# A graph layer's convolution by frequencies: the shared product in fp32, the other factors' sums from the table, three buffers

## What is computed

```python
h = relu(bn1(conv1d(h, conv1_w)))            # one tap
h = bn2(conv1d(h, conv2_w, pad=8))           # 17 taps over the 256 nodes, 256 -> 256 channels
x_conv = relu(h + x)
x_nmp  = exp(-dist(x)) @ relu(x @ w_msg.T + b_msg)
gi = concat(x_conv, x_nmp) @ w_ih.T + b_ih   # then the gates of a GRU cell
```

## Time and profile before

| | |
|---|---|
| median of three runs | 1865.35 us |
| the profiled execution, its own time | 1863.11 us |
| its span in the profile | 1861.2 us |
| PE busy | 1794.3 us (96%) |
| PE weight loads busy | 1603.6 us (86%) |
| DVE busy | 1296.5 us (70%) |
| ACT busy | 1058.2 us (57%) |
| POOL busy | 972.0 us (52%) |
| DMA moved | 262.65 MB |

### The profile page before, as it was taken

The page is one execution under the profiler, slowest core; times in us unless marked ns, Lnnn a source line. Parts: engine busy times, 40 slices in busy tenths (PEclk is TensorE's granted clock), DMA queues, the critical chain, the costliest instruction groups (busy, mean ns, idle before and its releaser), DMA issues.

```text
span 1861.2 us, 31300 instructions
## 1 busy us (share of the span) xinstructions
PE 1794.3 (96%) x10736; PEld 1603.6 (86%) x10736; DVE 1296.5 (70%) x2316; ACT 1058.2 (57%) x1883; POOL 972.0 (52%) x1092
## 2 busy tenths in 40 slices
PE   5999999999999998999879999999999999999998
PEld 5999999999999998999768888888888888888886
DVE  8899999999888729999984454454455455445444
ACT  5998989989898876666543233233333323323322
POOL 6788888888767629999951222122122122212211
PEclk9999999999999999999989999999999999999999
DMA  6465665656555355665754534544443453454442
GB/s 199 140 213 190 206 197 197 209 189 212 203 187 183 136 160 133 146 168 145 191 156 123 118 78 102 119 83 102 114 92 93 113 114 80 104 119 82 101 109 40
DMA packets 513819, 262.65 MB, mean 141 GB/s; under 512 B 365575, under 2 KB 473479, under 8 KB 513662
## 3 DMA queue, kind: packets, MB, share of 16 engines
q1 hardware_dynamic: 512606, 260.52, 50.9%
q10 hardware_dynamic: 1056, 0.13, 0.0%
HBM read 151.51 MB, written 109.05 MB: 140 GB/s over the span
## 4 chain that ended last, share of the span: by engine, by line
PE 84%; DVE 6%; issue 4%; POOL 3%; DMA 2%; ACT 1%; SPq 0%; DVEq 0%; POOLq 0%; ACTq 0%
PE P L114 70%; PE P L936 5%; PE P L619 4%; PE P L646 3%; PE P L638 1%; DVE yo L829 1%; DVE wh0l L774 1%; DMA y_d<-yo 1%; POOL xsum L727 1%; PE P L667 1%; DVE wsum L755 1%; DVE wh1l L774 1%; POOL xh1l L745 0%; ACT mt L817 0%; DVE wgl L893 0%
## 5 line engine op out<-in xcount | busy, mean ns | idle before, releaser
L918 POOL TENSOR_TENSOR xnx1l<-xnf,xnx1h 128x1024 fp32r<-128x1024 f32 x16 | 44.4, 2773 | 344.3 <-ACT xnx1h L911 344.3
L918 POOL TENSOR_TENSOR xnx0l<-xnf,xnx0h 128x1024 fp32r<-128x1024 f32 x15 | 41.6, 2774 | 318.4 <-ACT xnx0h L911 318.4
L1017 ACT ACTIVATE tr<-P,cold 128x512 f32<-128x512 f32 x64 | 44.2, 690 | 194.2 <-PE P L114 194.2
L1020 ACT ACTIVATE nn<-gn,col 128x512 f32<-128x512 f32 x64 | 46.4, 725 | 179.3 <-DVE gn L1034 179.3
L1041 DVE SCALAR_TENSOR_TENSOR tz<-tz,tr 128x512 f32<-128x512 f32 x64 | 44.3, 692 | 147.9 <-ACT tz L1024 147.8
L549 POOL TENSOR_TENSOR axl<-af,axh 128x512 fp32r<-128x512 f32 x64 | 92.2, 1441 | 99.4 <-ACT axh L375 99.4
L1024 ACT ACTIVATE tz<-P,cold 128x512 f32<-128x512 f32 x64 | 44.0, 688 | 162.1 <-PE P L114 162.1
L1030 DVE SCALAR_TENSOR_TENSOR gn<-tr,gn 128x512 f32<-128x512 f32 x64 | 44.2, 690 | 127.3 <-ACT tr L1017 127.3
L114 PE MATMUL P<-w1mh,xxh 128*128 128x512 f32 x256 | 108.0, 422 | 0.0
L936 PEld LDWEIGHTS P<-gt,yt 128*128 128x128 f32 x768 | 98.8, 189 | 6.8 <-DMA yt<-y_d 1.9
L936 PE MATMUL P<-gt,yt 128*128 128x136 f32 (+1 forms) x768 | 100.9, 281 | 1.5 <-DMA yt<-y_d 1.5
(11 more groups left out here) (227 smaller groups left out, 7119.7 us busy)
## 6 DMA issues: line engine op xcount, KB each, us to landing
xh_d<-xst SPq DMA_DIRECT2D x64, 320.0 KB, 4.9
xl<-xh_d SPq DMA_DIRECT2D x40, 512.0 KB, 6.2
y_d<-yo SPq DMA_DIRECT2D x80, 256.0 KB, 2.4
x<-in_x SPq DMA_DIRECT2D x64, 256.0 KB, 3.0
a<-in_adj SPq DMA_DIRECT2D x64, 256.0 KB, 4.2
at<-in_adjt SPq DMA_DIRECT2D x64, 256.0 KB, 4.6
x_d<-x SPq DMA_DIRECT2D x64, 256.0 KB, 4.7
xn_d<-xt SPq DMA_DIRECT2D x64, 256.0 KB, 4.8
```

Of the source, the lines that this page charges most:

```text
L918: e.e.tensor_tensor(o[1][:, :, :], xnf[p % 2][:, :, :, :].rearrange("p c i t -> p c (i t)"), o[0][:, :, :], ALU.subtract).then_inc(done, 1)
L1020: e.e.activation(nn[:, :], gn[:, :], ACT.Tanh, bias=n_b[:, o:o + 1]).then_inc(S["nn"], 1)
```

## The change

The common product is no longer made of split operands: it is one fp32 matmul for each c, of `xsum` and `wsum` themselves, two in place of six. The sums' high and low parts go away (`xsh`, `wsh` semaphores, L735, L745, L764, L774), and `xh`, `wh` hold two quantities in place of three. The table now gives -(wr + wi) and wi - wr, both factors of the other two products; `wsum` is -1 times the first minus the second, which is 2 wr, so the copy out of PSUM multiplies by 0.5. `wh`, `xsum` and `wsum` have three buffers, `yo` four. Both chunks' copies to `mt` are on ACT. `spectra_sum` and `weights_sum` wait for the bin that last used their buffer, no longer for the splits. The common product now comes before the waits for the split operands and for `ye`. The filter's operands are made two bins ahead, at the end of a turn.

```diff
-        v = np.cos(2 * np.pi * k * f / NT)
-        if im:
-            v = np.sin(2 * np.pi * k * f / NT) - v
+        re, imag = np.cos(2 * np.pi * k * f / NT), np.sin(2 * np.pi * k * f / NT)
+        v = re if f in (0, NF) else imag - re if im else -imag - re
...
-        xh = [p2.hl(f"xh{i}", [128, 3, 2, 256]) for i in range(3)]
-        wh = [p2.hl(f"wh{i}", [128, 3, 2, 256]) for i in range(2)]
-        xsum = p2("xsum", [128, 32, 16])
-        wsum = p2("wsum", [128, 2, 256])
+        xh = [p2.hl(f"xh{i}", [128, 2, 2, 256]) for i in range(3)]
+        wh = [p2.hl(f"wh{i}", [128, 2, 2, 256]) for i in range(3)]
+        xsum = [p2(f"xsum{i}", [128, 2, 256]) for i in range(3)]
+        wsum = [p2(f"wsum{i}", [128, 2, 256]) for i in range(3)]
         mt = [p2(f"mt{i}", [128, 256]) for i in range(2)]
-        yo = [p2(f"yo{i}", [128, 512]) for i in range(2)]
+        yo = [p2(f"yo{i}", [128, 512]) for i in range(4)]
...
         def spectra_sum(e, f):
+
             e.wait_ge(S[f"lxh{f // 2 % 2}"], 2 * loaded(f // 2, 2))
-            e.wait_ge(S["xslo"], f - 1)
-            e.wait_ge(S["xshi"], f - 1)
+            e.wait_ge(S["frq"], 2 * f - 4)
             x = bin_of(f)
-            e.e.tensor_tensor(xsum[:, :, :], x[:, 0], x[:, 1], ALU.add).then_inc(S["xsum"], 1)
+            e.e.tensor_tensor(xsum[f % 3][:, :, :].rearrange("p c (g t) -> p (c g) t", g=16), x[:, 0], x[:, 1],
+                              ALU.add).then_inc(S["xsum"], 1)
 
         def spectra_hi(e, f):
             e.wait_ge(S[f"lxh{f // 2 % 2}"], 2 * loaded(f // 2, 2))
             e.wait_ge(S["frq"], 2 * f - 4)
-            e.e.copy(parts_of(xh[f % 3][0]), bin_of(f)).then_inc(S["xhi"], 1)
-            if f:
-                e.wait_ge(S["xsum"], f)
-                e.e.copy(sum_of(xh[f % 3][0]), xsum[:, :, :]).then_inc(S["xshi"], 1)
+            e.e.copy(by_group(xh[f % 3][0]), bin_of(f)).then_inc(S["xhi"], 1)
 
         def spectra_lo(e, f):
             h, l = xh[f % 3]
             e.wait_ge(S["xhi"], f + 1)
             e.wait_ge(S["frq"], 2 * f - 4)
-            e.e.tensor_tensor(parts_of(l), bin_of(f), parts_of(h), ALU.subtract).then_inc(S["xlo"], 1)
-            if f:
-                e.wait_ge(S["xshi"], f)
-                e.wait_ge(S["xsum"], f)
-                e.e.tensor_tensor(sum_of(l), xsum[:, :, :], sum_of(h), ALU.subtract).then_inc(S["xslo"], 1)
+            e.e.tensor_tensor(by_group(l), bin_of(f), by_group(h), ALU.subtract).then_inc(S["xlo"], 1)
 
         def weights_of(f):
             return wf[f // 10 % 2][:, 2 * (f % 10):2 * (f % 10) + 2, :, :]
 
         def weights_sum(e, f):
             e.wait_ge(S["wev"], UNITS * (f // 10 + 1))
-            e.wait_ge(S["wslo"], f - 1)
-            e.wait_ge(S["wshi"], f - 1)
+            e.wait_ge(S["frq"], 2 * f - 4)
             w = weights_of(f)
-            e.e.scalar_tensor_tensor(out=wsum[:, :, :], in0=w[:, 0, :, :], scalar=-2.0, in1=w[:, 1, :, :],
+            e.e.scalar_tensor_tensor(out=wsum[f % 3][:, :, :], in0=w[:, 0, :, :], scalar=-1.0, in1=w[:, 1, :, :],
                                      op0=ALU.mult, op1=ALU.subtract).then_inc(S["wsum"], 1)
 
         def weights_hi(e, f):
             e.wait_ge(S["wev"], UNITS * (f // 10 + 1))
-            e.wait_ge(S["frq"], 2 * f - 2)
-            e.e.copy(wh[f % 2][0][:, 0:2, :, :], weights_of(f)).then_inc(S["whi"], 1)
-            if f:
-                e.wait_ge(S["wsum"], f)
-                e.e.copy(wh[f % 2][0][:, 2, :, :], wsum[:, :, :]).then_inc(S["wshi"], 1)
+            e.wait_ge(S["frq"], 2 * f - 4)
+            e.e.copy(wh[f % 3][0][:, :, :, :], weights_of(f)).then_inc(S["whi"], 1)
 
         def weights_lo(e, f):
-            h, l = wh[f % 2]
+            h, l = wh[f % 3]
             e.wait_ge(S["whi"], f + 1)
-            e.wait_ge(S["frq"], 2 * f - 2)
-            e.e.tensor_tensor(l[:, 0:2, :, :], weights_of(f), h[:, 0:2, :, :], ALU.subtract).then_inc(S["wlo"], 1)
-            if f:
-                e.wait_ge(S["wshi"], f)
-                e.wait_ge(S["wsum"], f)
-                e.e.tensor_tensor(l[:, 2, :, :], wsum[:, :, :], h[:, 2, :, :], ALU.subtract).then_inc(S["wslo"], 1)
+            e.wait_ge(S["frq"], 2 * f - 4)
+            e.e.tensor_tensor(l[:, :, :, :], weights_of(f), h[:, :, :, :], ALU.subtract).then_inc(S["wlo"], 1)
 
 
         def main(chunk):
@@ -782,51 +762,46 @@
 
         def freq(e, f, chunk):
 
+
             n = 2 * f + chunk
+            xb, wb = xh[f % 3], wh[f % 3]
+
+            def product(o, q, k):
+                return multiply(e.e, mm3([{c: x[:, q, c, 128 * chunk:128 * chunk + 128] for c in range(2)} for x in xb],
+                                         [{c: w[:, k, c, :] for c in range(2)} for w in wb],
+                                         o, True, True, [(0, 0), (1, 1)]))
+
+            if f:
+                e.wait_ge(S["xsum"], f)
+                e.wait_ge(S["wsum"], f)
+                e.wait_ge(S["mt"], n - 3)
+                for c in range(2):
+                    t = e.e.matmul(common(chunk)[:, 0:256], xsum[f % 3][:, c, 128 * chunk:128 * chunk + 128],
+                                   wsum[f % 3][:, c, :], start=c == 0, stop=c == 1, skip_group_check=True)
+                t.then_inc(S["com"], 1)
             e.wait_ge(S["xhi"], f + 1)
             e.wait_ge(S["xlo"], f + 1)
             e.wait_ge(S["whi"], f + 1)
             e.wait_ge(S["wlo"], f + 1)
             e.wait_ge(S["ye"], n - 1)
-            e.wait_ge(S[f"mt{chunk}"], f - 1)
-            xb, wb = xh[f % 3], wh[f % 2]
-
-            def product(o, q, k):
-                return multiply(e.e, mm3([{c: x[:, q, c, 128 * chunk:128 * chunk + 128] for c in range(2)} for x in xb],
-                                         [{c: w[:, k, c, :] for c in range(2)} for w in wb],
-                                         o, True, True, [(0, 0), (1, 1)]))
-
-            if f == 0:
-                product(main(chunk)[:, 0:256], 0, 0)
-                product(main(chunk)[:, 256:512], 1, 1).then_inc(S["frq"], 1)
-                return
-            e.wait_ge(S["xshi"], f)
-            e.wait_ge(S["xslo"], f)
-            product(common(chunk)[:, 0:256], 2, 0).then_inc(S["com"], 1)
-            product(main(chunk)[:, 256:512], 0, 1)
-            e.wait_ge(S["wshi"], f)
-            e.wait_ge(S["wslo"], f)
-            product(main(chunk)[:, 0:256], 1, 2).then_inc(S["frq"], 1)
+            product(main(chunk)[:, 0:256], 1 if f else 0, 0)
+            product(main(chunk)[:, 256:512], 0 if f else 1, 1).then_inc(S["frq"], 1)
 
         def common_out(e, f, chunk):
-
             n = 2 * f + chunk
             e.wait_ge(S["com"], n - 1)
             e.wait_ge(S["ye"], n - 1)
-            if chunk == 0:
-                e.e.copy(mt[0][:, :], common(0)[:, 0:256]).then_inc(S["mt0"], 1)
-            else:
-                e.e.tensor_copy(mt[1][:, :], common(1)[:, 0:256]).then_inc(S["mt1"], 1)
+            e.e.mul(mt[chunk][:, :], common(chunk)[:, 0:256], 0.5).then_inc(S["mt"], 1)
 
         def freq_out(e, f, chunk):
             n = 2 * f + chunk
             e.wait_ge(S["frq"], n + 1)
-            e.wait_ge(S[f"sy{chunk}"], 16 * f)
+            e.wait_ge(S[f"sy{n % 4}"], 16 * (n // 4))
             if f == 0:
-                e.e.tensor_copy(yo[chunk][:, :], main(chunk)[:, :]).then_inc(S["ye"], 1)
+                e.e.tensor_copy(yo[n % 4][:, :], main(chunk)[:, :]).then_inc(S["ye"], 1)
                 return
-            e.wait_ge(S[f"mt{chunk}"], f)
-            e.e.tensor_tensor(yo[chunk][:, :].rearrange("p (q o) -> p q o", q=2),
+            e.wait_ge(S["mt"], n - 1)
+            e.e.tensor_tensor(yo[n % 4][:, :].rearrange("p (q o) -> p q o", q=2),
                               main(chunk)[:, :].rearrange("p (q o) -> p q o", q=2),
                               mt[chunk][:, :].unsqueeze(1).broadcast_to((128, 2, 256)),
                               ALU.add).then_inc(S["ye"], 1)
...
 
         def load_y(e, b):
             e.wait_ge(S["idf"], b - 2)
-            e.wait_ge(S[f"sy{b // 32}"], 16 * NF)
+            for n in (b // 32, b // 32 + 2):
+                e.wait_ge(S[f"sy{n}"], 16 * (2 * NF // 4))
             e.e.dma_start(yt[b % 3][:, 0:2, :], y_all[4 * NT * b:4 * NT * b + 384].rearrange(
...
                 unit_out(e, n)
-            weights_hi(e, 0)
+            for f in range(2):
+                weights_hi(e, f)
             for n in range(UNITS, UNITS + AHEAD):
                 unit_out(e, n)
             spectra_hi(e, 1)
             for f in range(NF):
-                if f + 1 < NF:
-                    weights_hi(e, f + 1)
                 if f:
                     common_out(e, f, 0)
                 if f + 2 < NF:
                     spectra_hi(e, f + 2)
                 for n in units_in(f, 0):
                     unit_out(e, n)
+                if f:
+                    common_out(e, f, 1)
                 for n in units_in(f, 1):
                     unit_out(e, n)
+                if f + 2 < NF:
```

(24 more changed lines are left out.)

## The result

The changed kernel took 1836.71 us (median of 4 runs, 1835.93 to 1838.8) against 1864.89 us of the kernel before in the same comparison: 0.9848 of its time, 95% interval 0.9831 to 0.9865. Forecast were 1836 us and a faster kernel. The span of the profiled execution went from 1861.2 to 1834.8 us, 26.4 us less; forecast were 29. (By median the two kernels are 28.2 us apart; the profiled execution of the kernel before took 1863.11 us, less than its median.)

The account below looks back on a forecast made before the run. DVE and POOL, both full at 6.72 us a bin in the middle stage, were taken as the bound. From 1863.11 us, -4.8, -10.0, -15.5 and +1.3 (together -29.0) gave 1834 profiled, 1836 us as median; range 1826 to 1850.

Parts of the forecast that it names:

- What bounds the kernel: Middle stage: DVE and POOL are both full, 6.72 us a bin; after the change they need 4.5 and 4.91.
- PE's part: Middle stage, each chunk: six split matmuls (0.72 us) give way to an fp32 pair (0.87 us), 0.30 us more a bin.
- The other view: Fp32 pair on PE priced as four split matmuls each: 0.96 us, 7 us more over the stage.
- Bins 2 to 29: Middle stage: 28 bins at 4.78 us plus 402 filter records at 0.11, 178.0 us for 188.05, a gain of 10.0.
- the signs: Expected traces: bins 2 to 8 at 6.3 us, 10 to 28 at 6.6, 9, 19 and 29 at 4.8, gate bins 6.2.
- Start: PE's first matmul of the middle stage to bin 1's eviction: bin 1 evicted at 711.05 for 715.81, a gain of 4.8 us.
- Behind what things wait: Middle stage: eviction behind the next low part is a 5.5 us chain, needed at 7.4, so it fits; buffers cost no time.
- The last ten bins: Bins 30 to 39: four at 4.8 us, six gate bins at 6.2 with DVE full; 55.4 us for 70.9, 15.5 gained.
- the rival of DVE and POOL keeping each other out: Last ten bins: no overlap of the two, 5.5 us a bin, 61.3 us in place of 55.4, 1842 us; chance 0.15.
- The clock: Gate bins: PE idles by a fifth, so some of the lower clock stays, +1.3 us, an estimate.
- The rival of the loads: Last bins: spectra loads bind, five pairs lose some 1 to 2 us each, 1844 us; chance 0.08.

Follow-up runs that it names:

- the second experiment: Changed kernel with the filter's operands made one bin ahead at the head of a turn, `wh` and `wsum` in two buffers; 1836.6 us.
- the one with both edits: Changed kernel with the gates' weight splits handed to other turns and each spectra load issued one turn earlier; 1832.42 us.
- loads earlier: Changed kernel with each load of two bins' spectra issued one turn earlier; 1832.77 us.
- block between: Changed kernel with each gate block's low part on DVE moved between the two evictions of the next bin; 1833.43 us.
- spread: Changed kernel with the six gate-weight splits in turns 29, 31, 33, 35 and two in 38, in place of 32 to 37; 1829.81 us.
- spread and between: Changed kernel with gate-weight splits in turns 29, 31, 33, 35 and 38, the first four moved between the next bin's evictions; 1828.86 us.
- POOL light: Changed kernel with POOL's low part of the spectrum made for a sixteenth of the columns in bins 32 to 39; 1825.45 us.

## Why the prediction was right

**What bounds the kernel.** Right. DVE and POOL set 6.72 us a bin: with their work put back, the time is back (0.9991). They got shorter by more than what was taken off, though: 15.5 and 16.5 us busy of 27 are some 3.6 and 3.8 us a bin, where 4.5 and 4.91 were forecast. POOL's sum has a median of 1.30 us now for 2.09 before, DVE's filter sum 0.69 for 1.12. The instructions left were priced as they last while both engines are full, and they are shorter once they meet less often.

**PE's part.** Right, and to 0.01 us: 0.217 us a record of 128 rows was read from records of 96 rows, and doubling the product cost 1.73 us a bin for the 1.74 forecast. The other view, the fp32 matmul as four split ones (0.96 us for the pair), would have made that 1.92, and is refuted. The four passes of the Trainium skill (FP8 and Floating Point Precision, TensorE Precision Notes) may be what PE does, but here they don't cost four times the pace of a split matmul: an fp32 matmul, two records, takes 0.43 us, a split one 0.12.

**Bins 2 to 29.** 176.5 us for 178.0, by two errors that cancel in part. A bin without units takes 4.60 us (evictions 889.43 and 894.03), not 4.78; so the filter's records cost (176.46 - 28 x 4.60) / 402 = 0.119 us, not the 0.11 I took from one bin; the 0.16 a bin that I added behind the filter's records is the same time, put in the wrong place. With many records a bin is at 6.74, with few at 6.0: with units it is as close to no gain as was said, and much of what was won lies at the start, in the bins without units and in the last ten. Of the signs, bins 2 to 8 took 6.26 us for 6.3. Bins 9, 19 and 29 took 5.55, not 4.8, since eviction to eviction they still hold the eight filter records behind the bin before, and bin 10 took 5.3.

**Start.** 9.87 us for 9.7.

**Behind what things wait.** That the eviction's new place behind the low part of bin f + 2 costs nothing with units was right: PE waits for no eviction before bin 34. That the buffers cost nothing fits the runs; that the filter's third buffers are not needed I had not said, and the second experiment shows it. For those of `xsum` and `yo` it is open.

**The last ten bins** are the term that was mis-sized: 59.7 us for 56.7. I took L893 at 1.7 us and DVE's turn with it at 6.2. It measured 2.21 us in the mean, 3.1 at the longest, because the rival of DVE and POOL keeping each other out holds in those bins: the block meets POOL's low part. The six gate bins took 6.8 us in the mean. I had the lock as all or nothing, 5.5 us for every bin; that is refuted in bins 30 and 31 (4.6 and 4.9 us), and its 61.3 us for the stretch was nearer than my figure for a reason that I had not separated. A bin's lock time depends on which instructions meet. PE's waits in the changed kernel show two long ones, the third being 1.40:

```profile
912.35 0.55 PE L113 MATMUL P<-wh1h,xh1h 128*128 128x256 f32 x1 [3.70 <-DVE yo L804]
...
938.95 0.50 PE L113 MATMUL P<-wh2h,xh2h 128*128 128x256 f32 x1 [3.20 <-DVE yo L804]
```

The first stands behind these two on DVE, which overlap POOL's L733:

```profile
906.30 2.31 DVE L754 TENSOR_TENSOR wh1l<-wf,wh1h 128x1024 fp32r<-128x1024 f32 x1
908.54 3.07 DVE L869 TENSOR_TENSOR wgl<-st_wg,wgh 128x768 fp32r<-128x768 f32 x1
```

```profile
907.49 3.29 POOL L733 TENSOR_TENSOR xh2l<-xl,xh2h 128x1024 fp32r<-128x1024 f32 x1
```

DVE's block ends at 911.61, 0.83 us after POOL's L733 (910.78).

**The clock** is the other part of that miss. The sum had 1.3 us for it. After each of the two long waits PE ran at the lower level, with its split matmuls 0.21 us apart for 0.12; against the upper level (1.51 us from the end of a wait to the next product, 2.30 from product to product) it lost 2.8 and 1.5 us. On the first occasion DVE was nearly as late anyway; by DVE's waits for PE behind them (0.47 and 1.89 us) some 2 us of the 4.3 reached the total. That is an estimate; it leaves some 2 us of the 3.0 to DVE's turn. The clock is also most of what separates the changed kernel from the one with both edits, whose waits are as long in all. Times in us, the waits from 889 to 950 us (last row: 940 to 1005):

| kernel | bins 30 to 39 | PE's waits for evictions | stretches at the lower clock |
|---|---|---|---|
| changed | 59.7 | 8.3 | two |
| no filter lead | 60.4 | 7.3 | two |
| loads earlier | 55.7 | 6.9 | one |
| block between | 56.3 | 6.1 | one |
| spread and loads earlier | 55.2 | 8.2 | none |
| spread | 51.6 | 4.0 | none |
| spread and between | 51.8 | 4.9 | none |
| POOL light | 47.8 | 1.3 | none |
| fp32 product twice | 63.2 | none | none |

**The number.** That 1836 us was met to 0.7 us is in part luck. From PE's first matmul to bin 39 27.4 us were won where 29.0 were forecast, the stage began 1.7 us later and the last stage was 0.7 us shorter, and executions of the kernel before differ by 5 us.

**The rival of the loads** was wrong in its mechanism though its waits came true: POOL waits 37 us for loads, and PE waits for evictions only. Still, issuing them earlier won 4 us in the last bins, by moving POOL's work against DVE's and by the clock, as far as the traces show.

## What to carry to other kernels

When two engines are full and a third nearly so, work can be taken off the full ones at the nearly full one's cost; price that cost from the nearest shape's start-to-start pace, not from durations, and stop where the third becomes the bound. Test "work or buffers" with the work put back into tiles that nobody reads: it costs one run and settles it. And where DVE and GpSimd both read SBUF, a DVE instruction's cost in a sum is a range (here 0.9 to 3.1 us for the same block); put optional DVE blocks where GpSimd waits or where DVE has free turns, and check what GpSimd's work will meet before making it punctual. A wait of PE can cost twice, once as a wait and once as the lower clock behind it.

## What the hardware showed that I had not expected

- Two edits that each win do not add: spread blocks 1829.8 us, earlier loads 1832.8, both 1832.4. At the place shown the early load puts POOL's work on top of DVE's.
- The length of a wait alone did not decide the clock: with earlier loads it fell behind a wait of 2.16 us, with both edits it stayed up behind one of 2.99.
- The first split matmul behind a group of fp32 records starts 0.31 us before the next (865.59 to 865.90) where 0.12 is usual in these rows, but the group itself is as much too short in the records (0.68 us from its start to that matmul, for 4 x 0.217 = 0.87). The two together, 0.99 us, are what four fp32 records and one split one cost, so a price read from that one gap would be wrong.
